# A two-layer graph/LSTM kernel: ScalarE instead of VectorE applies the first layer's normalisation, fused with its relu

## The chip, the cores and the metric

The kernel runs on one core of a Trainium2 chip. The metric is the device time of one execution in microseconds (us). The kernel before took 428.32 us, the median of 3 runs (428.17 to 431.04).

## The reference, cut to what matters

The input `x` is 64 batches of 128 rows (t) by 128 columns. Two layers with a residual follow each other; all of it is fp32.

```python
h = jnp.maximum(_layernorm(x, axis=-1), 0.0)          # the part that the change touches
x = x + _L0_gnn_ref(h, adj, Wg0, bg0, Wg1, bg1, Wih, Whh, bih, bhh)
h = jnp.maximum(_layernorm(x, axis=-1), 0.0)
x = x + _L1_gnn_ref(h, L1_W, adj, L1_bias)

# _L0_gnn_ref
h = relu(einsum('ts,bsh->bth', adj, x @ Wg0 + bg0))
h = relu(einsum('ts,bsh->bth', adj, h @ Wg1 + bg1))
for p in (1, 2, 3, 4):                                 # an LSTM over windows of p rows
    last = _lstm_last(Wih[p-1], Whh[p-1], bih[p-1], bhh[p-1], windows of p rows of h)
    h = h.at[:, every p-th row, :].set(last)
```

`_L1_gnn_ref` multiplies by three weight matrices, mixes the rows with the diagonal, the upper and the lower part of `adj`, and adds a bias.

## The kernel before, in words

**Groups and streams.** The 64 batches are worked off in 4 groups of 16. A group is split into two streams of 8 batches (s = 0 and 1) that alternate, so that one stream's matmuls run while the other stream's gates go through ScalarE and VectorE. `X` holds all of the input in SBUF; `H0` holds the normalised input of one group.

**Units.** The LSTM of a group is a list of 22 units (`UNITS`), k = 0 to 21, which all engines work off in the same order. A unit is one time step of one stream for one window length p: units 0 to 3 have p = 1, 4 to 7 p = 2, 8 to 13 p = 3 (336 columns) and 14 to 21 p = 4 (256 columns). Even k is stream 0 and odd k stream 1. Units 14 and 15 are the first steps of p = 4 and have three gates (input, cell, output); units 16 to 21 have four.

**What one unit does.** TensorE computes the gates into PSUM: first three matmuls per gate with the inputs `HH` and `HL` (high and low parts, L461, L462, L468), then, for a later step, three per gate with the state `SH` and `SL` (L477, L478, L481). The first L481 matmul of a unit waits for `SL` of the stream's previous unit. ScalarE applies sigmoid or tanh to each gate in turn (`GT`, L697), then, when VectorE has made the cell state `CS` (L808, or L811, L814 and L817), it takes its tanh (`TC`, L706). VectorE multiplies it with the output gate (`HT` or `HF`, L839) and makes the high part (L843) and the low part (L851). Every engine issues strictly in the order of its own program; nothing is rescheduled. VectorE calls `unit_cell` of units 1, 2 and 15 early (`CELL_EARLY`): for unit 15, the cell state comes ahead of `unit_low(14)`, which writes the `SL` that unit 16 needs.

**What is threaded between the units.** While group i is in its units, the layer norm of group i + 1 is prepared: VectorE takes the statistics after units 4 to 9 (L746), combines them at unit 10 (L753 to L765), and GpSimd makes `RS1` (one over the standard deviation, `rstd`, L320). Then VectorE applies it: at each of units 12 to 19 (`LN_APPLY_AT`), between `unit_cell` and `unit_hidden`, `norm_h0` (L771) computes (X + MINUS1) * RS1 for two batches. ScalarE applies the relu in place on eight batches at once (`relu_h0`, L632) after units 15 and 19 (`LN_RELU_AT`). Groups 0, 1 and 2 have a group to prepare (`more`); group 3 has none. For group 0's own batches, and for half of the second layer norm, ScalarE already makes normalisation and relu in one instruction per batch with `scale=RS` and `bias=SHIFT` (L674 and `norm_relu_h3`, L659).

**The last layer of the previous group.** From group 1 on, the second layer's work for group i - 1 is threaded into group i's units by a table (`Plan.at`): at (k, m), ahead of gate m of unit k, TensorE makes the mixed rows of one batch into PSUM (`last_uk`, L505 or L507 to L509), ScalarE copies them to `UK` (`copy_uk`, L665), and TensorE multiplies them by the weights (`last_out`, L522). All of these mixed rows go through one PSUM bank: at (15, 2) TensorE's `last_uk` of batch 15 waits until the copy of batch 14 is done, and ScalarE issues that copy at (15, 0), right after the tanh of unit 14. Group 0 has no such pieces.

## Time and profile before

| | |
|---|---|
| median of 3 runs | 428.32 us (428.17 to 431.04) |
| the profiled execution, its own time | 427.95 us |
| its span on the core | 425.6 us |
| mean granted TensorE clock | 0.992 of full speed |
| busy: TensorE matmul | 408.7 us (96%) |
| busy: VectorE | 328.8 us (77%) |
| busy: ScalarE | 279.9 us (66%) |
| busy: GpSimd | 48.2 us (11%) |

Busy time is the sum over an engine's instructions, without the gaps; a matmul's end is modelled, so a busy TensorE may still be kept from starting the next one on time. The span is what the trace covers; the execution's own time is 2.35 us longer. In the trace, PE is TensorE (PEld its weight loads), ACT is ScalarE, DVE is VectorE, POOL is GpSimd. Tiles appear under shortened names: H stands for H0 and H3, SHIFT for SHIFT1 and SHIFT2, RS for RS1 and RS2. Durations of neighbouring instructions on one engine overlap: where one starts less than its duration after the one before, the difference of the starts is what it occupies.

### The profile page before, as it was taken

Reading aid. Unit: us, or ns where it says so; the run is one execution under the profiler, and the core shown is the slowest. Engines: PE = TensorE matmul, PEld = TensorE weight load, DVE = VectorE, ACT = ScalarE, POOL = GpSimd, SP = SyncE. Lnnn points to the kernel's source line nnn. Section 1 sums busy time; section 2 is a strip of 40 time slices with the busy share of each in tenths; the row PEclk is TensorE's granted clock in tenths of the full one; section 3 lists DMA queues with packets and bytes.
Section 4 is the critical chain, followed back from the end, with each engine's and each line's share of the span. In section 5 each row is a group of like instructions: output and inputs, shape, how many; then the busy total and the mean of one; then the engine's idle time right before and its main releaser. Section 6 shows DMA issues by size and latency. Waiting matters only on the chain.

```text
span 425.6 us, 7802 instructions
## 1 busy us (share of the span) xinstructions
PE 408.7 (96%) x2594; PEld 366.6 (86%) x2594; DVE 328.8 (77%) x845; ACT 279.9 (66%) x566; POOL 48.2 (11%) x55
## 2 busy tenths in 40 slices
PE   8997989899999999999989999999999999999897
PEld 7785879898878889999867889999887889999787
DVE  5669888998886788887967678888888777767841
ACT  4667666765966576776766566767596676667542
POOL 3693002000200002000110001100110000000300
PEclk9998989999999999999999999999999999999999
DMA  7900000000001000000001000000000000000011
GB/s 217 375 28 1 2 0 2 1 2 0 2 19 39 14 0 15 1 20 2 0 2 37 32 0 12 1 18 0 1 2 19 27 0 14 0 20 0 9 55 63
DMA packets 6080, 11.16 MB, mean 26 GB/s; under 512 B 1056, under 2 KB 4768, under 8 KB 5536
## 3 DMA queue, kind: packets, MB, share of 16 engines
q1 hardware_dynamic: 6048, 10.77, 7.1%
q8 instruction: 16, 0.26, 0.2%
q14 instruction: 16, 0.13, 0.1%
HBM read 6.57 MB, written 4.19 MB: 25 GB/s over the span
## 4 chain that ended last, share of the span: by engine, by line
PE 82%; DVE 8%; ACT 4%; issue 3%; DMA 1%; POOL 1%; SPq 0%; DVEq 0%; ACTq 0%
PE PS L468 11%; PE PS L461 11%; PE PS L462 11%; PE PS L522 8%; PE PS L481 6%; PE PS L478 6%; PE PS L477 6%; PE PS L505 5%; PE PS L394 3%; PE PS L417 3%; PE PS L409 3%; PE PS L427 3%; ACT GT L697 2%; PE PS L491 1%; ACT TC L706 1%
## 5 line engine op out<-in xcount | busy, mean ns | idle before, releaser
L697 ACT ACTIVATE GT<-PS,BG 128x256 f32<-128x256 f32 (+2 forms) x312 | 159.1, 563 | 55.4 <-PE PS L481 31.2
L461 PE MATMUL PS<-HH,WIH 128*128 128x256 f32 (+2 forms) x312 | 109.9, 352 | 7.3 <-DVE HH L843 3.6
L468 PE MATMUL PS<-HL,WIH 128*128 128x256 f32 (+2 forms) x312 | 104.6, 335 | 0.4
L462 PE MATMUL PS<-HH,WIL 128*128 128x256 f32 (+2 forms) x312 | 104.2, 334 | 0.0
L706 ACT ACTIVATE TC<-CS 128x512 f32<-128x512 f32 (+2 forms) x88 | 45.1, 512 | 44.1 <-DVE CS L817 28.9
L461 PEld LDWEIGHTS PS<-HH,WIH 128*128 128x128 f32 x312 | 59.9, 192 | 12.2 <-DVE HH L843 4.3
L320 POOL TENSOR_TENSOR RS<-VE,NHALF 128x8 f32<-128x8 f32 (+2 forms) x15 | 26.5, 1766 | 350.9 <-DVE VE L765 350.9
L468 PEld LDWEIGHTS PS<-HL,WIH 128*128 128x128 f32 x312 | 59.8, 192 | 7.0 <-DVE HL L851 2.4
L462 PEld LDWEIGHTS PS<-HH,WIL 128*128 128x128 f32 x312 | 60.0, 192 | 3.5
L481 PE MATMUL PS<-SL,WHH 128*128 128x256 f32 (+2 forms) x192 | 59.8, 311 | 0.0
L478 PE MATMUL PS<-SH,WHL 128*128 128x256 f32 (+2 forms) x192 | 59.8, 311 | 0.0
L477 PE MATMUL PS<-SH,WHH 128*128 128x256 f32 (+2 forms) x192 | 59.7, 311 | 0.0
L522 PEld LDWEIGHTS PS<-WL,UK 128*128 128x128 f32 x384 | 50.9, 191 | 5.4
L522 PE MATMUL PS<-WL,UK 128*128 128x128 f32 x384 | 52.5, 275 | 0.0
L665 ACT ACTIVATE UK<-PS 128x384 f32<-128x384 f32 x64 | 31.0, 485 | 12.7 <-PE PS L509 8.9
L811 DVE TENSOR_TENSOR IC<-GT 128x256 f32<-128x256 f32 (+2 forms) x48 | 23.9, 498 | 19.1 <-ACT GT L697 18.9
L839 DVE TENSOR_TENSOR HF<-GT,TC 128x512 f32<-128x512 f32 (+2 forms) x40 | 24.6, 614 | 16.9 <-ACT TC L706 16.0
L478 PEld LDWEIGHTS PS<-SH,WHL 128*128 128x128 f32 x192 | 36.3, 189 | 1.3
L477 PEld LDWEIGHTS PS<-SH,WHH 128*128 128x128 f32 x192 | 36.3, 189 | 1.3
L481 PEld LDWEIGHTS PS<-SL,WHH 128*128 128x128 f32 x192 | 36.3, 189 | 1.3
L808 DVE TENSOR_TENSOR CS<-GT 128x512 f32<-128x512 f32 (+2 forms) x40 | 24.9, 622 | 12.4 <-ACT GT L697 10.2
L839 DVE TENSOR_TENSOR HT<-GT,TC 128x256 f32<-128x256 f32 (+2 forms) x48 | 23.8, 497 | 12.6 <-ACT TC L706 12.4
(81 smaller groups left out, 577.0 us busy)
## 6 DMA issues: line engine op xcount, KB each, us to landing
X<-x_tbd SPq DMA_DIRECT2D x3, 1024.0 KB, 12.5
out_tbd<-X SPq DMA_DIRECT2D x15, 192.0 KB, 1.9
X<-x_tbd SPq DMA_DIRECT2D x4, 256.0 KB, 4.5
WI<-wih_t SPq DMA_DIRECT2D x1, 1024.0 KB, 6.8
out_tbd<-X SPq DMA_DIRECT2D x7, 128.0 KB, 1.7
WH<-whh_t SPq DMA_DIRECT2D x1, 768.0 KB, 8.6
out_tbd<-X SPq DMA_DIRECT2D x1, 256.0 KB, 2.0
WL<-w_l SPq DMA_DIRECT2D x1, 192.0 KB, 7.0
```

Source lines behind the costliest of these rows:

```text
L320: pool.tensor_tensor(rs[:, lo:hi], ve[:, lo:hi], NHALF[:, lo:hi], ALU.pow).then_inc(done, 1)
L461: pe.matmul(dst, WIH[:, p - 1, cols], x_high, start=True, stop=False)
L462: pe.matmul(dst, WIL[:, p - 1, cols], x_high, start=False, stop=False)
L468: mm = pe.matmul(dst, WIH[:, p - 1, cols], x_low, start=False, stop=(j == 0))
L477: pe.matmul(dst, WHH[:, p - 2, cols], SH[:, s, 0:n], start=False, stop=False)
L478: pe.matmul(dst, WHL[:, p - 2, cols], SH[:, s, 0:n], start=False, stop=False)
L481: pe.matmul(dst, WHH[:, p - 2, cols], SL[:, s, 0:n], start=False, stop=True).then_inc(gate_mm, 1)
L522: mm = pe.matmul(as_batches(ps)[:, n - plan.chunks[c][0], :], UK[:, n % 4, k * T:(k + 1) * T], WL1[:, k, :], start=False, stop=(k == ADJ_P ...
L665: act.activation(UK[:, n % 4, :], ps[:, 0:ADJ_PARTS * T], ACT.Copy).then_inc(uk_sb, 1)
L697: act.activation(GT[:, s, q, 0:n], bank(s, q)[:, 0:n], ACT.Tanh if q == C else ACT.Sigmoid, bias=BG[:, 4 * (p - 1) + q:4 * (p - 1) + q + 1 ...
L706: act.activation(TC[:, s, 0:n], CS[:, s, 0:n], ACT.Tanh).then_inc(tanh_ready, 1)
L839: dve.tensor_tensor(full, o, tc, ALU.mult).then_inc(lstm_step, 1)
```

## The change

`norm_h0` on VectorE and `relu_h0` on ScalarE go. In their place ScalarE has `norm_relu_h0`: after the tanh of each of units 12 to 19 it makes relu(X * RS1 + SHIFT1) for two batches, one instruction per batch. GpSimd makes `SHIFT1` = MINUS1 * RS1 for the whole group with one more instruction behind its `RS1`. TensorE's wait ahead of the next group's first matmuls now counts batches (`h0_ready` is raised 16 times a group instead of 2). Nothing else moves.

```diff
-LN_RELU_AT = {15: 0, 19: 1}
...
             def group(i, more):
                 if more:
                     rstd(VE1, var1, 2 * (QUARTERS + i + 1), RS1, rs1, 0, G)
+                    pool.wait_ge(rs1, QUARTERS + i + 1)
+                    pool.tensor_tensor(SHIFT1[:, :], MINUS1[:, :], RS1[:, :], ALU.mult).then_inc(shift1, 1)
...
                 if not first:
-                    pe.wait_ge(h0_ready, STREAMS * (g - 1) + s + 1)
+                    pe.wait_ge(h0_ready, G * (g - 1) + HB * (s + 1))
...
         def _(act):
-            def relu_h0(s, g):
-
-                act.wait_ge(norm1, G * (g - 1) + HB * (s + 1))
-                part = H0[:, s * HB:(s + 1) * HB, :]
-                act.activation(part, part, ACT.Relu).then_inc(h0_ready, 1)
+            def norm_relu_h0(g, batches):
+
+                act.wait_ge(shift1, QUARTERS + g)
+                for b in batches:
+                    act.activation(H0[:, b, :], X[:, g * G + b, :], ACT.Relu, bias=SHIFT1[:, b:b + 1],
+                                   scale=RS1[:, b:b + 1]).then_inc(h0_ready, 1)
...
             def units(i, more, plan):
                 for k in range(len(UNITS)):
                     unit(k, i, plan)
-                    if more and k in LN_RELU_AT:
-                        relu_h0(LN_RELU_AT[k], i + 1)
+                    if more and k in LN_APPLY_AT:
+                        norm_relu_h0(i + 1, LN_APPLY_AT[k])
...
         def _(dve):
-            def norm_h0(g, ready, batches):
-
-                dve.wait_ge(rs1, ready)
-                for b in batches:
-                    dve.tensor_scalar(H0[:, b, :], X[:, g * G + b, :], MINUS1[:, b:b + 1], RS1[:, b:b + 1],
-                                      ALU.add, ALU.mult).then_inc(norm1, 1)
...
-                    if more and k in LN_APPLY_AT:
-                        norm_h0(i + 1, QUARTERS + i + 1, LN_APPLY_AT[k])
                     unit_hidden(k, i)
```

ScalarE in group 0, from the tanh of unit 13 (`TC`, 336 columns) to that of unit 16, before:

```order
L706 ACTIVATE TC<-CS 128x336
L697 ACTIVATE GT<-PS,BG 128x256 x3
L706 ACTIVATE TC<-CS 128x256
L697 ACTIVATE GT<-PS,BG 128x256 x3
L706 ACTIVATE TC<-CS 128x256
L632 ACTIVATE H<-H 128x1024
L697 ACTIVATE GT<-PS,BG 128x256 x4
L706 ACTIVATE TC<-CS 128x256
```

and the same stretch in the changed kernel, whose line numbers are by one or two different:

```order
L707 ACTIVATE TC<-CS 128x336
L632 ACTIVATE H<-X,SHIFT,RS 128x128 x2
L698 ACTIVATE GT<-PS,BG 128x256 x3
L707 ACTIVATE TC<-CS 128x256
L632 ACTIVATE H<-X,SHIFT,RS 128x128 x2
L698 ACTIVATE GT<-PS,BG 128x256 x3
L707 ACTIVATE TC<-CS 128x256
L632 ACTIVATE H<-X,SHIFT,RS 128x128 x2
L698 ACTIVATE GT<-PS,BG 128x256 x4
L707 ACTIVATE TC<-CS 128x256
```

Two small instructions stand behind every tanh, ahead of the next unit's gates; the large one behind unit 15 is gone. In groups 1 and 2 the same happens, and there the copy of batch 14 (`UK`) stands behind them too. ScalarE there, from the tanh of unit 14 on, before:

```order
L706 ACTIVATE TC<-CS 128x256 [waits cell_ready]
L664 REGISTER_ALU
L665 ACTIVATE UK<-PS 128x384 [waits uk_mm]
```

and changed, where the ISA rows are register work that the moving batch address needs:

```order
L707 ACTIVATE TC<-CS 128x256 [waits cell_ready]
L632 ISA [waits shift1]
L632 ACTIVATE H<-X,SHIFT,RS 128x128
L632 ISA
L632 ACTIVATE H<-X,SHIFT,RS 128x128
L665 REGISTER_ALU
L666 ACTIVATE UK<-PS 128x384 [waits uk_mm]
```

The copy, which came right behind the tanh, now has two instructions ahead of it. VectorE in group 0, from the high part of unit 13 (`HH`, L843) to that of unit 14, before:

```order
L843 CAST HH<-HF 128x42x8
L851 TENSOR_TENSOR HL<-HF,HH 128x42x8
L808 TENSOR_TENSOR CS<-GT 128x256
L771 TENSOR_SCALAR H<-X,MINUS,RS 128x128 x2
L839 TENSOR_TENSOR HT<-GT,TC 128x256
L843 CAST SH<-HT 128x256
L808 TENSOR_TENSOR CS<-GT 128x256
L851 TENSOR_TENSOR SL<-HT,SH 128x256
```

and changed:

```order
L837 CAST HH<-HF 128x42x8 [waits lstm_step]
L845 TENSOR_TENSOR HL<-HF,HH 128x42x8 [waits lstm_step]
L802 TENSOR_TENSOR CS<-GT 128x256 [waits gate_act]
L833 TENSOR_TENSOR HT<-GT,TC 128x256 [waits tanh_ready]
L837 CAST SH<-HT 128x256 [waits lstm_step]
L802 TENSOR_TENSOR CS<-GT 128x256 [waits gate_act]
L845 TENSOR_TENSOR SL<-HT,SH 128x256 [waits lstm_step]
```

The pair L771 is gone and nothing has changed places: the cell state of unit 15 (the second `CS`) still stands ahead of the `SL` of unit 14, and waits for ScalarE's gates (`gate_act`).

## Rows read from the trace of the kernel before

**Rows 1.** The page, busy time: busy us, share of the span, instructions.

```profile
PE 408.7 (96%) x2594; PEld 366.6 (86%) x2594; DVE 328.8 (77%) x845; ACT 279.9 (66%) x566; POOL 48.2 (11%) x55
```

**Rows 2.** The page, the chain that ended last, by engine.

```profile
PE 82%; DVE 8%; ACT 4%; issue 3%; DMA 1%; POOL 1%; SPq 0%; DVEq 0%; ACTq 0%
```

**Rows 3.** Groups of instructions by line and shape: busy us, mean ns | idle us before.

```profile
L632 ACT ACTIVATE H<-H 128x1024 f32<-128x1024 f32 x6 | 6.4, 1060 | 0.7 <-DVE H L771 0.4
L659 ACT ACTIVATE H<-X,SHIFT,RS 128x128 f32 x16 | 6.4, 481 | 0.5 <-POOL SHIFT L377 0.5
...
L771 DVE TENSOR_SCALAR H<-X,MINUS,RS 128x128 f32 x32 | 9.6, 341 | 0.0
```

**Rows 4.** Timeline of ScalarE in group 1: start us, length us, count.

```profile
209.71 0.86 ACT L659 ACTIVATE H<-X,SHIFT,RS 128x128 f32 x2
```

**Rows 5.** Line L659 alone: register work between its instructions, ns min/median/max.

```profile
L659 ACTq FUSED_REGOPS  x16: 51/55/60, 207.3 to 309.8; - x16
```

**Rows 6.** Timeline of ScalarE in group 1, the tanh of unit 12, then units 13 to 15.

```profile
169.71 0.48 ACT L706 ACTIVATE TC<-CS 128x336 f32<-128x336 f32 x1 [0.66 <-DVE CS L817]
...
173.41 0.48 ACT L706 ACTIVATE TC<-CS 128x336 f32<-128x336 f32 x1 [0.18 <-DVE CS L817]
173.80 1.19 ACT L697 ACTIVATE GT<-PS,BG 128x256 f32<-128x256 f32 x3
175.72 0.42 ACT L706 ACTIVATE TC<-CS 128x256 f32<-128x256 f32 x1 [0.73 <-DVE CS L808]
176.08 0.49 ACT L665 ACTIVATE UK<-PS 128x384 f32<-128x384 f32 x1
```

**Rows 7.** Timeline of VectorE in group 1, unit 14.

```profile
175.27 0.42 DVE L808 TENSOR_TENSOR CS<-GT 128x256 f32<-128x256 f32 x1
175.60 0.60 DVE L771 TENSOR_SCALAR H<-X,MINUS,RS 128x128 f32 x2
```

**Rows 8.** Timeline of TensorE, `last_uk` of batch 15 in group 1.

```profile
176.63 0.44 PE L507 MATMUL PS<-ADJ3H,H3H 128*128 128x384 f32 x1 [0.48 <-ACT UK L665]
```

**Rows 9.** Timeline of ScalarE in group 1, unit 17, the tanh of unit 19, the gates of unit 20.

```profile
183.84 1.57 ACT L697 ACTIVATE GT<-PS,BG 128x256 f32<-128x256 f32 x4 [0.32 <-PE PS L481]
186.00 0.42 ACT L706 ACTIVATE TC<-CS 128x256 f32<-128x256 f32 x1 [0.58 <-DVE CS L817]
...
191.73 0.42 ACT L706 ACTIVATE TC<-CS 128x256 f32<-128x256 f32 x1 [0.59 <-DVE CS L817]
...
193.21 1.55 ACT L697 ACTIVATE GT<-PS,BG 128x256 f32<-128x256 f32 x4
```

**Rows 10.** Timeline of VectorE in group 1, the low part of unit 19.

```profile
192.97 0.42 DVE L851 TENSOR_TENSOR SL<-HT,SH 128x256 fp32r<-128x256 f32 x1
```

**Rows 11.** Timeline of TensorE in group 1: unit 21's first L481, then the next group's first matmuls.

```profile
194.99 0.28 PE L481 MATMUL PS<-SL,WHH 128*128 128x256 f32 x1
...
196.18 1.95 PE L394 MATMUL PS<-ADJ,H 128*128 128x128 f32 x16
```

**Rows 12.** Timeline of ScalarE in group 0, the tanh of unit 13.

```profile
76.04 0.48 ACT L706 ACTIVATE TC<-CS 128x336 f32<-128x336 f32 x1 [0.66 <-DVE CS L817]
```

**Rows 13.** Timeline of VectorE in group 0, CS of unit 15, SL of unit 14.

```profile
79.52 0.42 DVE L808 TENSOR_TENSOR CS<-GT 128x256 f32<-128x256 f32 x1
79.86 0.42 DVE L851 TENSOR_TENSOR SL<-HT,SH 128x256 fp32r<-128x256 f32 x1
```

**Rows 14.** Timeline of TensorE in group 0: unit 15's start, first L481 of units 16 and 21.

```profile
77.49 0.39 PE L461 MATMUL PS<-HH,WIH 128*128 128x256 f32 x1 [1.65 <-DVE HH L843]
...
80.64 0.28 PE L481 MATMUL PS<-SL,WHH 128*128 128x256 f32 x1
...
95.00 0.28 PE L481 MATMUL PS<-SL,WHH 128*128 128x256 f32 x1
```

**Rows 15.** Timeline of GpSimd in group 1.

```profile
163.12 3.11 POOL L320 TENSOR_TENSOR RS<-VE,NHALF 128x16 f32<-128x16 f32 x1 [48.24 <-DVE VE L765]
...
207.06 0.20 POOL L377 TENSOR_TENSOR SHIFT<-MINUS,RS 128x8 f32<-128x8 f32 x1
```

More of the change, by code:

```diff
@@ L208, in program @@
         shift1 = sem("shift1")
-        norm1 = sem("norm1")
         h0_first = sem("h0_first")
```

## The prediction

> **What bounds the kernel now.** I read the page's busy times first, then the chain that ended last, then the groups by line and shape to price the instructions, and last the timelines of ScalarE, VectorE and TensorE around units 12 to 21, where the change works. TensorE is busy for 408.7 of 425.6 us [rows 1], and it holds 82% of the chain that ended last, ScalarE 4% and VectorE 8% [rows 2]. So a few us that leave VectorE give nothing by themselves, and a few that come to ScalarE cost nothing by themselves. What counts is whether TensorE's next matmul is held up by something that ScalarE does later than before. The reader should look for the places where TensorE already waits in this stretch: in group 1 for ScalarE's copy of batch 14, 0.48 us [rows 8] (group 2 has the same wait), and in group 0 for unit 13's high part, 1.65 us [rows 14]. Where TensorE waits for the very engine that gets work, there is no slack.
>
> **Removed.** Three groups have a successor. Each loses sixteen VectorE instructions of 341 ns, of which two take 0.60 us, thus eight pairs, and two ScalarE relu of 1.06 us [rows 3, 7]. The pairs stand between the cell state and the hidden state, where VectorE waits for the tanh anyway: the pair from 175.60 to 176.20 lies beside the tanh from 175.72 to 176.14 [rows 6, 7]. I count 0 gained, with the second rival below as the other end.
>
> **Added.** Sixteen ScalarE instructions per group. The nearest row is the same form on the same engine in the second layer norm: 481 ns each [rows 3], two in 0.86 us, so the second starts 0.38 us after the first [rows 4]. A pair then occupies 2 x 0.385 = 0.77 us. There is 55 ns of register work with each of them [rows 5], which the two in 0.86 us hide. Upper bound for a pair: no overlap and the register work in the open, 2 x (0.48 + 0.055) = 1.07 us. Lower bound: 0.76, two of the closest spacing that a row of this form shows. I take 0.77, because these rows are the same instruction in the same kind of loop. ScalarE gets 8 x 0.77 = 6.2 us per group and loses 2 x 1.06 = 2.1.
>
> Two instructions over 1024 columns become sixteen over 128: by [rows 3] an eighth of the columns still takes 0.48 of 1.06 us, so small pieces are dear here. The Trainium skill speaks against this change: "ScalarE: Activation LUTs", section "Rules for kernel authors", sends relu, add and mul to VectorE and not to ScalarE. By the durations the trace agrees, 341 ns there against 481 ns here; by that rule the change loses, and the third rival says how much it could lose at most. Whether TensorE waits for it the rule doesn't say.
>
> GpSimd gets one small product behind RS1. RS1 is out at 163.12 + 3.11 = 166.23 us, and a product of half the columns takes 0.20 us [rows 15]. Even at twice that, SHIFT1 is there by 166.8, and ScalarE first asks for it behind the tanh of unit 12, at 170.1 [rows 6]: no cost, and no gain either. TensorE's changed wait counts the sixteenth batch, ready behind unit 19, well before its use at 196.18 [rows 11]: no cost either, as long as ScalarE's lag stays as small as worked out below.
>
> **Groups 1 and 2: the copy of batch 14.** I walk ScalarE with the starts of group 1 [rows 6]. Behind unit 12 a pair takes up the time in which ScalarE waited for unit 13's gates, all but 0.05 us. So the tanh of unit 13 is at 173.46 instead of 173.41. The next instruction may start 0.39 later (173.80 - 173.41), and the pair pushes it by 0.77: gates of unit 14 at 174.62 instead of 173.80. The cell gate is the second of three that take 1.19 us together, so it ends some 0.83 later, at 175.45. VectorE makes CS from it at 175.48 instead of 175.27, when it had been held by its own earlier work [rows 7]. 0.42 later and 0.03 on, the tanh of unit 14 starts at 175.93 instead of 175.72. Then 0.36 and the second pair, 0.77: the copy starts at 177.06 instead of 176.08, that is 0.98 us later. The first delay is half swallowed by VectorE, the second not at all. TensorE's L507 already waits for this copy [rows 8], so it moves by the whole 0.98, and everything behind it in TensorE's program too. Group 2 repeats group 1. Together 1.96 us.
>
> **Groups 1 and 2: the lag that builds up afterwards,** measured against the shifted TensorE. ScalarE was idle for 0.32 us ahead of unit 17's gates [rows 9] and could have started 0.06 sooner still (a tanh takes 0.42, and the next starts 0.36 behind it [rows 6]). A pair of 0.77 there makes those gates 0.39 late. From gates to tanh are 186.00 - 183.84 = 2.16 us [rows 9], so with 0.36 and the pair a unit takes ScalarE 3.29 us. TensorE's unit takes 2.87 (24 matmuls; in these rows unit 20's gates would follow unit 17's by three of them, but for the relu). Each further unit adds 0.42: unit 18 is 0.81 late, unit 19 1.23. Unit 19's SL is out at 192.97 + 0.42 + 1.23 = 194.62 [rows 10], and TensorE needs it at 194.99 [rows 11]: 0.37 us of slack left, no stall. Behind unit 19 a pair replaces a longer relu, so unit 20's gates are at most 1 us late: 193.21 + 1.55 + 1.0 = 195.8, before the next group's matmuls at 196.18 ask for them. After that no pair follows, and ScalarE catches up. Cost 0; if the cover were gone, each 0.1 us more per pair costs unit 19's SL 0.3 us.
>
> **Group 0** has no pieces of the last layer. Here the late gates of unit 15 act through VectorE, which makes CS of unit 15 ahead of unit 14's SL. Tanh of unit 13 at 76.09 [rows 12], gates of unit 14 at 76.09 + 0.39 + 0.77 = 77.25, cell gate out at 78.08, CS at 78.11, tanh of unit 14 at 78.56, gates of unit 15 at 78.56 + 0.36 + 0.77 = 79.69, cell gate out at 80.52. So CS of unit 15 is at 80.55 instead of 79.52, SL of unit 14 stands 0.34 behind it as before [rows 13], at 80.89, and is out at 81.31. TensorE wanted it at 80.64 [rows 14]: a new stall of 0.69 us. Then the lag: tanh of unit 15 at 81.00, gates of unit 16 at 82.13, of unit 19 three periods of 3.29 later at 92.00, its tanh at 94.16, its SL 1.24 behind (192.97 against 191.73 [rows 9, 10]) at 95.40, out at 95.82. TensorE needs it at 95.00 + 0.69 = 95.69 [rows 14]: another 0.13. Group 0 costs 0.8 us.
>
> **Sum.** 0.8 + 2 x 0.98 = 2.8 us. The profiled execution took 427.95 us, 2.35 more than its span of 425.6; the same one would take 430.7 with a span of 428.4. The median of the runs shown lies 0.37 above the profiled one: 431.1 us, 0.6% slower.
>
> **The rivals.** First, slower by over 1%: a pair costs more than 0.77 us because the second instruction or the gates behind it don't overlap. At the upper bound of 1.07 the two pairs ahead of the copy make it 0.98 + 0.6 = 1.58 late; the lag is 0.69 at unit 17 and grows by 0.72, so unit 19's SL comes 0.5 after 194.99: 2.1 for each of groups 1 and 2. In group 0 unit 14's SL costs 1.3 and unit 19's another 1.3. Together 6.8 us: 435.1. Between 2.8 at 0.77 and 6.8 at 1.07 the bound of 1% (4.3 us) is passed at a pair of 0.88 us. For it: every pair stands behind a tanh and ahead of instructions that read PSUM, which the two of [rows 4] also do only in part. Against: they overlap all the same.
>
> Second, not slower: VectorE's pairs were what TensorE waited for, and their going gives back what ScalarE costs or more. If all of the waits in the stretch went (1.65 + 2 x 0.48 = 2.6 us), the time would be 425.7; if they only made up for my 2.8, 428.3. For it: VectorE starts its hidden states right behind a pair. Against: the tanh ends as the pair does, so its going releases nothing, and the copy of batch 14 doesn't depend on VectorE at all once the tanh is out.
>
> Third, all of the added occupancy counts, since ScalarE becomes the bound: 3 x (6.2 - 2.1) = 12.3 us, 440.6. That is the most that the rule of the skill named above could mean here. For it: with 3.29 us a unit ScalarE is slower than TensorE in units 16 to 19. Against: it is so for four units only, then it catches up, and over the span it is busy for 66% [rows 1].
>
> **How the numbers follow.** Chances: my forecast 0.68 (429 to 432.6), the dearer pair 0.18, no cost or a gain 0.11, all of it 0.03. The range of 428.6 to 434.2 reaches down into the second rival and up to a pair of about 1.0 us. A measurement of this kernel can tell about 1% from no change, here 4.3 us. Slower by more than that (above 432.6): the first and third rival and 0.01 of mine, 0.22. Faster by more than that needs more than all of TensorE's waits in the stretch: 0.03. Within 1%: 0.75.
>
> **What would show it.** In the profile of the changed kernel: pairs of 0.86 us on ScalarE behind each tanh of units 12 to 19; the L507 of batch 15 waiting for UK for about 1.4 us in groups 1 and 2; in group 0 a wait of TensorE for SL of about 0.7 us at unit 16; no idle time on ScalarE ahead of the gates of units 17 to 20; no new wait at the matmuls that open the next group; a span of 428.4. I am wrong if TensorE waits by more than 0.3 us for SL or SH in units 18 to 21 of groups 1 and 2, or if the copy's wait stays below 0.6.

## The result, and the profile after

| | before | changed |
|---|---|---|
| median of 20 runs each, us | 428.21 (425.75 to 431.04) | 431.48 (429.22 to 433.2) |
| profiled execution, us | 427.95 | 432.27 |
| its span, us | 425.6 | 430.1 |
| mean granted clock of that execution | 0.992 | 0.987 |

The ratio is 1.0065 (95% interval 1.005 to 1.008): the changed kernel is 0.65% slower, where 431.1 us was forecast. That is less than the 1% (4.3 us) that the prediction took as the least that can be told from no change, but the interval excludes no change. The times of both kernels spread with the granted clock, so medians and single spans are not the cleanest measure of some us. Grouped by mean granted clock, the executions at 0.992 have a mean span of 425.8 us before (44 executions, from the rounds of the experiments) and 428.6 changed (11): 2.8 us. Side by side in experiment 10 it is 425.8 (14) against 428.5 (seven). One execution of the kernel before, beside experiments 1 to 4, took 571.06 us at a clock of 0.656 and is left out everywhere. The changed kernel's profiled execution carries 1.5 us beside that, which the clock section at the end places.

The busy times and the chain's shares of the changed kernel's page, which answer to [rows 1, 2], and ScalarE's group for the new instructions:

```profile
PE 410.4 (95%) x2594; PEld 368.1 (86%) x2594; DVE 318.4 (74%) x797; ACT 290.7 (68%) x608; POOL 47.8 (11%) x58
PE 78%; DVE 10%; ACT 7%; issue 2%; DMA 1%; POOL 1%; ACTq 0%; SPq 0%; DVEq 0%
L632 ACT ACTIVATE H<-X,SHIFT,RS 128x128 f32 x32 | 13.9, 480 | 0.0
L632 ACT ACTIVATE H<-X,SHIFT,RS 128x128 f32<-128x128 f32 x16 | 6.9, 480 | 0.0
```

VectorE lost 10.4 us of busy time and ScalarE gained 10.8. No view of the chain shows a bound that moved: TensorE still holds 78% of it. But ScalarE's share went from 4 to 7%, and each of its 48 new instructions takes 480 ns, with no idle time ahead of it.

ScalarE in group 1 of the changed kernel, its timeline from unit 13's tanh to unit 21's gates, as [rows 6, 9] (start, duration, engine, instruction, in brackets the idle time ahead and what ended it):

```profile
174.30 0.48 ACT L707 ACTIVATE TC<-CS 128x336 f32<-128x336 f32 x1 [0.18 <-DVE CS L811]
174.69 0.86 ACT L632 ACTIVATE H<-X,SHIFT,RS 128x128 f32 x2
175.46 1.18 ACT L698 ACTIVATE GT<-PS,BG 128x256 f32<-128x256 f32 x3
176.76 0.42 ACT L707 ACTIVATE TC<-CS 128x256 f32<-128x256 f32 x1
177.08 0.86 ACT L632 ACTIVATE H<-X,SHIFT,RS 128x128 f32 x2
177.85 0.47 ACT L666 ACTIVATE UK<-PS 128x384 f32<-128x384 f32 x1
...
184.82 0.42 ACT L707 ACTIVATE TC<-CS 128x256 f32<-128x256 f32 x1 [0.59 <-DVE CS L811]
185.15 0.86 ACT L632 ACTIVATE H<-X,SHIFT,RS 128x128 f32 x2
185.92 1.55 ACT L698 ACTIVATE GT<-PS,BG 128x256 f32<-128x256 f32 x4
188.05 0.42 ACT L707 ACTIVATE TC<-CS 128x256 f32<-128x256 f32 x1 [0.58 <-DVE CS L811]
...
195.59 1.54 ACT L698 ACTIVATE GT<-PS,BG 128x256 f32<-128x256 f32 x4
```

From a pair's start to the next instruction it is 0.77 us at each of the three places (174.69 to 175.46, 177.08 to 177.85, 185.15 to 185.92). The copy of batch 14 (`UK`) starts at 177.85. From the tanh of unit 16 (184.82) to that of unit 17 it is 3.23 us, and the only idle time of ScalarE in a unit is the 0.58 in which it waits for the cell state.

TensorE in the changed kernel, its timeline at the places of [rows 8, 14]; the second line is group 1, the third group 2:

```profile
76.90 0.38 PE L461 MATMUL PS<-HH,WIH 128*128 128x256 f32 x1 [1.65 <-DVE HH L837]
...
178.37 0.44 PE L507 MATMUL PS<-ADJ3H,H3H 128*128 128x384 f32 x1 [1.33 <-ACT UK L666]
...
282.77 0.44 PE L507 MATMUL PS<-ADJ3H,H3H 128*128 128x384 f32 x1 [1.33 <-ACT UK L666]
```

The wait for the copy has grown from 0.48 to 1.33 us in both groups, and nothing new stands at units 18 to 21. In group 0 no wait for `SL` shows at unit 16 in this execution. Experiment 3's profile has one, and the clock section at the end says what differs.

**Where the time went.** The "graph stage" is the adjacency and weight matmuls that open a group, ahead of its units. I read the start of the same eight matmuls in each trace and take the differences. A is the first L461 of unit 15 in group 0 (behind its wait of 1.65), B the first L394 that follows (the opening of the next graph stage), C the first L461 of unit 9 in group 1 (behind a wait of 0.23), D the next L394 behind it; E is the third L505 of group 2 (it waits 1.56 for a copy before, 1.88 changed), F and G are C and D in group 2, H is the first L505 of the last group's own rows, near the end. In us:

| | A to B (group 0, units 15 to 21) | B to C | C to D (group 1) | D to E | E to F | F to G (group 2) | G to H |
|---|---|---|---|---|---|---|---|
| before | 18.71 | 58.41 | 41.57 | 22.60 | 37.60 | 41.52 | 103.56 |
| changed | 20.20 | 58.40 | 42.41 | 22.92 | 39.07 | 42.41 | 103.58 |

Groups 1 and 2 cost 0.84 and 0.89. The 1.49 of A to B and the 1.47 of E to F hold something else: the granted clock falls there, and it doesn't at the same places of the third and fifth experiments, which place group 0's cost at 0.72 + 0.23 = 0.95. The 0.32 of D to E is in this profile only: in experiment 10, the same kernel, D to E is 22.65.

### The profile page after: what moved, and what is told of

Same layout as the page of the kernel before. It is cut to its first block, busy times and chain, and to the rows that moved or that the text cites. A ratio compares the mean times of both kernels' runs of the same rounds, so it can differ in the third digit from the quotient of the medians.

```text
span 430.1 us, 7827 instructions
## 1 busy us (share of the span) xinstructions
PE 410.4 (95%) x2594; PEld 368.1 (86%) x2594; DVE 318.4 (74%) x797; ACT 290.7 (68%) x608; POOL 47.8 (11%) x58
## 4 chain that ended last, share of the span: by engine, by line
PE 78%; DVE 10%; ACT 7%; issue 2%; DMA 1%; POOL 1%; ACTq 0%; SPq 0%; DVEq 0%
PE PS L468 10%; PE PS L461 10%; PE PS L462 10%; PE PS L522 9%; PE PS L481 5%; PE PS L478 5%; PE PS L477 5%; PE PS L505 5%; ACT GT L698 4%; PE PS L427 3%; PE PS L394 3%; PE PS L417 3%; PE PS L409 3%; DVE CS L811 2%; DVE CS L808 2%
## 5 line engine op out<-in xcount | busy, mean ns | idle before, releaser
L461 PE MATMUL PS<-HH,WIH 128*128 128x256 f32 (+2 forms) x312 | 110.1, 353 | 8.0 <-DVE HH L837 7.5
L461 PEld LDWEIGHTS PS<-HH,WIH 128*128 128x128 f32 x312 | 60.3, 193 | 12.8 <-DVE HH L837 4.3
L481 PE MATMUL PS<-SL,WHH 128*128 128x256 f32 (+2 forms) x192 | 59.8, 311 | 0.0
L481 PEld LDWEIGHTS PS<-SL,WHH 128*128 128x128 f32 x192 | 36.3, 189 | 1.3
```

What stands on the lines that cost most here:

```text
L461: pe.matmul(dst, WIH[:, p - 1, cols], x_high, start=True, stop=False)
L481: pe.matmul(dst, WHH[:, p - 2, cols], SL[:, s, 0:n], start=False, stop=True).then_inc(gate_mm, 1)
```

## The experiments

Each ran in five rounds beside the kernel before, on the same chip as it (experiments 9 to 11 on another chip than 1 to 8; at a clock of 0.992 the kernel before has 425.8 us on both). "At equal clock" compares the mean spans of executions with the same mean granted clock. They are few in places, and the count stands beside each. "Period of ScalarE" below is the time from one unit's tanh to the next one's.

**1. The pair of unit 14 behind the copy** (groups 1 and 2 only).

```diff
+                    if plan is STEADY and k == 15 and m == 0:
+                        norm_relu_h0(i + 1, LN_APPLY_AT[14])
...
-                    if more and k in LN_APPLY_AT:
+                    if more and k in LN_APPLY_AT and not (plan is STEADY and k == 14):
```

> The changed kernel, but in the groups that carry last-layer pieces ScalarE issues the pair of unit 14 behind the copy of batch 14 and not ahead of it. Theory (ScalarE costs only where it stands ahead of something that TensorE waits for): the wait of TensorE's L507 for the copy shrinks from 1.33 us by one pair, 0.77, to 0.5 to 0.6 us in groups 1 and 2; the time falls by 1.5 us against the changed kernel, ratio to the kernel before about 1.003. Rival (all of ScalarE's added occupancy counts): nothing is removed, ratio stays at 1.0065. Rival (the loss is in the lag of units 16 to 19): stays at 1.0065 and TensorE shows waits there.

Measured: 430.44 us, ratio 1.0055 (1.0029 to 1.0082). TensorE at the copy in group 1:

```profile
179.44 0.44 PE L507 MATMUL PS<-ADJ3H,H3H 128*128 128x384 f32 x1 [0.58 <-ACT UK L666]
```

The wait is 0.58 instead of 1.33: the pair that stands directly ahead of the copy makes the 0.75 between them. C to D falls from 42.41 to 41.65, by 0.76. The median moved by less than that promises. Of this variant's 12 executions 9 had a mean clock of 0.988 or less, of the changed kernel's 12 of 32; at equal clock its span is 426.7 (0.992, two executions) and 428.3 (0.988, five), against 428.6 and 429.8 (three). So the work is 1.5 to 1.9 us shorter, and the clock takes a part of it back: the median fell by 1.0.

**2. All pairs away from the copy and from unit 15's gates.** The pairs of units 13 and 14 go behind units 11 and 15.

```diff
-LN_APPLY_AT = {12 + k: (2 * k, 2 * k + 1) for k in range(G // 2)}
+LN_APPLY_AT = {11: (0, 1), 12: (2, 3), 15: (4, 5, 6, 7), **{16 + k: (8 + 2 * k, 9 + 2 * k) for k in range(4)}}
```

> The changed kernel with the same sixteen instructions per group at other units: two batches behind each of units 11 and 12, none behind 13 and 14, four behind 15, two behind each of 16 to 19. Theory: no pair stands ahead of the copy of batch 14 (wait of L507 back at 0.5 us) and none delays the gates of units 14 and 15 (no stall for SL in group 0), ratio 1.000 to 1.001. Rival of the occupancy: the same 16 x 0.385 us are still on ScalarE, ratio 1.0065. Rival of the lag: the lag of units 16 to 19 is the same as before, ratio stays near 1.006.

Measured: 431.03 us, ratio 1.008 (1.0055 to 1.0106). The expectation was missed, and the median alone would say that the placement doesn't matter. The trace says otherwise: the copy's wait is down to what it was before,

```profile
179.59 0.44 PE L507 MATMUL PS<-ADJ3H,H3H 128*128 128x384 f32 x1 [0.42 <-ACT UK L666]
```

and no wait for `SL` is left. But 8 of its 9 executions had a clock of 0.988 or less. That made the ninth run necessary.

**3. VectorE's sixteen instructions put back.** They are issued at their old places, with their old operands and results, but write a part of Z that nothing reads; H0 still comes from ScalarE.

```diff
+            def norm_scr(g, ready, batches):
+
+                dve.wait_ge(rs1, ready)
+                for b in batches:
+                    dve.tensor_scalar(Z[:, b // HB, D * (b % HB):D * (b % HB) + D], X[:, g * G + b, :],
+                                      MINUS1[:, b:b + 1], RS1[:, b:b + 1], ALU.add, ALU.mult).then_inc(norm1, 1)
...
+                    if more and k in LN_APPLY_AT:
+                        norm_scr(i + 1, QUARTERS + i + 1, LN_APPLY_AT[k])
                     unit_hidden(k, i)
```

> The changed kernel with VectorE's sixteen instructions per group put back at their old places, writing to a tile that is dead at that time; nothing reads them. Theory (VectorE's relief gave nothing): equal to the changed kernel within 0.1%, ratio 1.006 to 1.007. Rival (VectorE's relief hid a part of ScalarE's cost): slower than the changed kernel, up to 1.012, with longer waits of TensorE for VectorE's SL or HH.

Measured: 430.75 us, ratio 1.007 (1.0044 to 1.0095); the profiled span is 428.4 at a clock of 0.992, where the changed kernel's mean at that clock is 428.6. With 11 us of VectorE work back (busy for 329.7 us, against 318.4), nothing became slower: their going had given back nothing. C to D is 42.42 (changed 42.41). This is also the trace in which group 0 can be read at an undisturbed clock. TensorE there, and the copy in group 1:

```profile
81.25 0.39 PE L482 MATMUL PS<-SL,WHH 128*128 128x256 f32 x1 [0.44 <-DVE SL L855]
...
178.43 0.44 PE L508 MATMUL PS<-ADJ3H,H3H 128*128 128x384 f32 x1 [1.34 <-ACT UK L667]
```

So the stall at unit 16 exists: 0.44 idle, and that matmul starts 3.77 behind A, where it was 3.15 before: 0.62. A to B is 19.43 against 18.71: 0.72. No lag is added to it at unit 21, whose first L482 uses unit 19's `SL`:

```profile
95.03 0.43 DVE L855 TENSOR_TENSOR SL<-HT,SH 128x256 fp32r<-128x256 f32 x1
95.72 0.28 PE L482 MATMUL PS<-SL,WHH 128*128 128x256 f32 x1
```

`SL` is out at 95.46, 0.26 ahead of its use. B to C is 58.64 against 58.41: 0.23 more, in the graph stage that follows, where the weight load of L418 (L417 before) waits 0.64 us for ScalarE's `Z` instead of 0.37.

**4. The copy of batch 14 ahead of unit 14's tanh,** which is an edit of the table that orders the pieces; the other copy of that row stays.

```diff
-        (13, 4): ((ADJP, 13),), (15, 0): both(14), (15, 2): both(15), (16, 1): ((OUTP, 15),)},
+        (13, 4): ((ADJP, 13),), (14, 3): ((ADJP, 14),), (15, 0): ((OUTP, 13),), (15, 2): both(15), (16, 1): ((OUTP, 15),)},
...
-        (13, 4): ((ADJP, 9),), (15, 0): both(10), (15, 2): both(11), (16, 1): ((OUTP, 11),)},
+        (13, 4): ((ADJP, 9),), (14, 3): ((ADJP, 10),), (15, 0): ((OUTP, 9),), (15, 2): both(11), (16, 1): ((OUTP, 11),)},
```

> The changed kernel with one entry of the table moved: the piece of batch 14 (in the last group batch 10) goes from ahead of unit 15's first gate to behind unit 14's last gate, so that ScalarE copies it ahead of unit 14's tanh and of the pair; TensorE's order is the same. Theory: the wait of L507 for the copy nearly goes (from 1.33 to under 0.2 us) in groups 1 and 2 and from 0.41 to under 0.1 in group 3, 2.6 us less for groups 1 and 2 at most, and ScalarE then lags by 1.2 us more behind TensorE in units 16 to 19, of which 0.1 to 0.4 us per group come back as waits for SL of unit 19; ratio 1.000 to 1.002. Rival of the occupancy: ratio stays at 1.006.

Measured: 428.63 us, ratio 1.0017 (0.9992 to 1.0041). ScalarE in group 1:

```profile
177.27 0.49 ACT L666 ACTIVATE UK<-PS 128x384 f32<-128x384 f32 x1
177.64 0.42 ACT L707 ACTIVATE TC<-CS 128x256 f32<-128x256 f32 x1
177.95 0.88 ACT L632 ACTIVATE H<-X,SHIFT,RS 128x128 f32 x2
```

The copy no longer stands behind tanh and pair, and no matmul shows a wait for it. But the weight load does, since the pair of unit 13 still makes gates and copy late:

```profile
177.81 0.19 PEld L507 LDWEIGHTS PS<-ADJ3H,H3H 128*128 128x128 f32 x1 [0.25 <-ACT UK L666]
```

C to D falls from 42.41 to 41.39; in experiment 7, with the same table edit and no pairs, it is 40.81. Group 0, which the edit doesn't reach, keeps its 0.72 (A to B 19.43). The span at 0.992 is 426.05 (six executions), which is 2.6 below the changed kernel.

**5. Unit 15's cell state behind unit 14's `SL`,** to take the wait for `SL` away from group 0.

```diff
-CELL_EARLY = (1, 2, 15)
+CELL_EARLY = (1, 2)
```

> The changed kernel with unit 15 taken out of the list of early cell states, so that VectorE makes the SL of unit 14 ahead of the CS of unit 15. Theory: the wait of TensorE for SL at unit 16 in group 0 (0.44 to 0.46 us in the traces where the clock did not hide it) goes, the two waits for the copy of batch 14 stay at 1.3 us; 0.5 us less than the changed kernel, which shows in the profile and hardly in the ratio (1.005 to 1.006). Rival (the stall comes from ScalarE's lag itself, not from the order on VectorE): the wait stays or moves to SH or SL of the same unit.

Measured: 430.97 us, ratio 1.0064 (1.0032 to 1.0095). The wait for `SL` at unit 16 is gone from the trace, and group 0 still costs 0.63 in A to B and 0.32 in B to C, 0.95 as in experiment 3. The 0.5 us that the expectation took off didn't come: at 0.992 the span is 428.45 (four), against 428.6. Taking the stall away gained nothing. ScalarE in this kernel, group 0:

```profile
75.67 0.87 ACT L632 ACTIVATE H<-X,SHIFT,RS 128x128 f32<-128x128 f32 x2
...
94.15 1.54 ACT L698 ACTIVATE GT<-PS,BG 128x256 f32<-128x256 f32 x4
```

The gates of unit 20 start 17.42 us behind A here (A is 76.73). In experiment 3, with the stall:

```profile
94.89 1.54 ACT L699 ACTIVATE GT<-PS,BG 128x256 f32<-128x256 f32 x4
```

that is 17.41 behind its A of 77.48. Before it was 16.41. ScalarE arrives equally late with and without the stall, since its own chain from unit 13 on sets it. And now TensorE reaches unit 21 early enough to be held there, its weight load by unit 19's `SL`, which it is not in experiment 3:

```profile
94.78 0.19 PEld L481 LDWEIGHTS PS<-SL,WHH 128*128 128x128 f32 x1 [0.16 <-DVE SL L845]
```

**6. A third instruction of the same form** behind units 16, 17 and 18, into a part of Z that nothing reads: extra work, to find out how much cover the lag has left.

```diff
+                        if k in (16, 17, 18):
+                            b = LN_APPLY_AT[k][0]
+                            act.activation(Z[:, 0, D * (k - 16):D * (k - 15)], X[:, (i + 1) * G + b, :], ACT.Relu,
+                                           bias=SHIFT1[:, b:b + 1], scale=RS1[:, b:b + 1]).then_inc(extra, 1)
```

> The changed kernel with one more instruction of the same form (0.385 us, into a tile that is dead at that time) behind each of units 16, 17 and 18. Theory (the lag of units 16 to 19 was covered with 0.37 us left in groups 1 and 2, with less than nothing left in group 0): 1.15 us more lag at unit 19, so 0.8 us per group in groups 1 and 2 and 1.1 in group 0, 2.7 us more than the changed kernel, ratio 1.012 to 1.013, with waits of TensorE for SL or SH of unit 19 at unit 21. Rival (ScalarE's occupancy is never on the path): no change, 1.0065. Rival (all occupancy counts, nothing was covered): 9 x 0.385 = 3.5 us more, 1.0145.

Measured: 435.53 us, ratio 1.0158 (1.0122 to 1.0194), six executions. TensorE now waits in the open at unit 21, in all three groups; the one of group 1:

```profile
198.90 0.39 PE L478 MATMUL PS<-SH,WHH 128*128 128x256 f32 x1 [0.23 <-DVE SH L844]
```

C to D and F to G are 43.15, both 0.74 above the changed kernel, where 0.8 was forecast; A to B is 0.76 above it. Three instructions are 1.16 us of ScalarE at 0.385 each; 0.74 of them reach TensorE within the units, so 0.4 us of cover was left there, as the prediction had it (0.37).

But most of the covered part is paid later, which the expectation didn't have. The stages behind the units are longer too: B to C by 0.36, G to H by 0.35, and D to E is 23.21, against 22.92 in the changed kernel's profile and 22.65 in experiment 10's. At a clock of 0.992 the span is 432.0 (two executions), 3.4 above the changed kernel. The theory had 2.7 and the rival "all occupancy counts" 3.5, so by the total the rival is nearer; by the stages it is wrong about where. By these two executions nearly all of the added time of ScalarE was paid, about two thirds of it in the units and the rest in the stage behind them.

**7. The kernel before, with only the table edit of experiment 4.**

> The kernel before with only the piece of batch 14 (batch 10 in the last group) moved behind unit 14's last gate, so that its copy comes ahead of unit 14's tanh. Theory: TensorE's three waits of 0.48, 0.42 and 0.41 us go, 1.2 us less than before at most, ratio 0.997 to 0.998. Rival (the copy delays the tanh and with it the chain of unit 14): ratio 1.000 or above.

Measured: **425.88 us, ratio 0.9944 (0.9917 to 0.9971)**, faster than the kernel before. ScalarE in group 1:

```profile
173.90 1.19 ACT L697 ACTIVATE GT<-PS,BG 128x256 f32<-128x256 f32 x3
174.97 0.50 ACT L665 ACTIVATE UK<-PS 128x384 f32<-128x384 f32 x1
175.82 0.42 ACT L706 ACTIVATE TC<-CS 128x256 f32<-128x256 f32 x1 [0.34 <-DVE CS L808]
```

The copy fits between the gates and the tanh, where ScalarE has nothing to do. C to D is 40.81, 0.76 below before; F to G 0.72, G to H 0.70 below. At a clock of 0.992 the span is 423.8 (six executions), 1.9 below before. Each of the three waits showed 0.41 to 0.48 us of idle TensorE and was worth 0.70 to 0.76; the expectation had counted the idle time alone. The rest is in rows beside it. TensorE's weight load before, in group 1:

```profile
176.62 0.19 PEld L507 LDWEIGHTS PS<-ADJ3H,H3H 128*128 128x128 f32 x1 [0.68 <-ACT UK L665]
```

The load itself had waited 0.68, and the matmul behind it takes 0.44 [rows 8], while in this experiment, unheld, it takes 0.34:

```profile
176.08 0.34 PE L507 MATMUL PS<-ADJ3H,H3H 128*128 128x384 f32 x1
```

Here each such wait cost 0.28 to 0.30 us beside its idle time.

**8. Experiment 2's placement and the table edit together.**

> The changed kernel with the pairs moved as in the run e2_pairs_moved and the copy of batch 14 moved as in e4_copy_ahead_of_tanh. Theory: no wait for the copy, no stall for SL of unit 14; 1.2 us less than the kernel before at an equal granted clock, ratio 0.997 to 0.999 if the clock drops as often as in the kernel before. In e2 the waits were gone as forecast, but the ratio was 1.008 and the mean granted clock 0.984 to 0.988 against 0.992 of the kernel before: if that belongs to the placement of the pairs, it repeats here and the ratio is 1.003 to 1.005; if it was that job's accident, the clocks are 0.992 again.

Measured: 427.37 us, ratio 0.9983 (0.9959 to 1.0006). At a clock of 0.992 its span is 424.7 (seven executions): 1.0 below before, 0.9 above experiment 7. In groups 1 and 2 that difference is not at the pairs behind units 15 to 19. C to D is 41.01, 0.2 above experiment 7, and all of it is there when unit 15 starts (20.53 behind C, against 20.32): with pairs behind both unit 11 and unit 12, the tanh of unit 13 is 0.2 late, and with it the `HH` that TensorE waits for. D to E is 0.19 above experiment 7; A to B holds a fall of the clock here and can't be read.

**9. Experiment 2 again, and 10. the changed kernel again,** with no edit to either, to see whether the median of experiment 2 was chance.

> The same kernel as e2_pairs_moved, to tell whether its extra clock drops belong to it. In e2 the profile had no wait that the kernel before has not, and all of its 3 us sat in two more drops of TensorE's clock (mean clock 0.984 to 0.988). If the drops belong to the placement of the pairs: clock again 0.984 to 0.988 in most runs and ratio 1.006 to 1.008. If they were chance: 0.992 in most runs and ratio 1.000 to 1.003; at an equal clock the span is within 0.5 us of the kernel before in either case.

> The changed kernel itself, beside the others on the same chip. Theory: ratio 1.006 to 1.008; at a mean clock of 0.992 its span is 2.8 us above that of the kernel before, of which 0.9 us lie in group 0 and 0.9 in each of groups 1 and 2.

Measured: 430.45 us, ratio 1.0048 (1.0023 to 1.0073), and 431.06 us, ratio 1.0073 (1.0042 to 1.0103). The intervals overlap: by their medians the two placements can't be told apart. By the stages they can: C to D and F to G are 41.71 (twice) in the ninth and 42.42 in the tenth, A to B 19.17 in the ninth, against 19.43 in experiment 3. And at a clock of 0.992 the spans are 427.1 (three) and 428.5 (seven). The placement of experiment 2 is worth 1.4 us at equal clock, and its executions get the lower clock in 8 of 12 cases. It is still 1.3 above before, where the expectation had at most 0.5: 0.46 in A to B and 0.31 in B to C, without a stall at unit 16, and 0.14 to 0.22 in each of C to D, D to E and F to G.

**11. Seven of the changed kernel's sixteen instructions ahead of a tanh instead of behind it,** with the table edit. The sixteen are the same; one each of units 12 and 16 to 21 is issued between the gates and the wait for the cell state. The other nine still stand behind a tanh: two at unit 11, one at 12, four at 15, one each at 16 and 17.

```diff
-LN_APPLY_AT = {12 + k: (2 * k, 2 * k + 1) for k in range(G // 2)}
+LN_APPLY_AT = {11: (0, 1), 12: (3,), 15: (4, 5, 6, 7), 16: (9,), 17: (11,)}
+LN_AHEAD_OF_TANH = {12: (2,), 16: (8,), 17: (10,), 18: (12,), 19: (13,), 20: (14,), 21: (15,)}
...
+                if plan is not LATE and k in LN_AHEAD_OF_TANH:
+                    norm_relu_h0(i + 1, LN_AHEAD_OF_TANH[k])
```

> ScalarE makes the same sixteen instructions per group, placed by where it stands idle: two behind unit 11's tanh, one ahead of and one behind unit 12's, four behind unit 15's, one ahead of each tanh of units 16 to 21, one more behind those of 16 and 17; the copy of batch 14 ahead of unit 14's tanh. Theory (the place decides, not the amount): ScalarE's idle time between a unit's last gate and its tanh, 0.58 us, takes an instruction of 0.385 us for nothing, so no lag builds up; no wait for the copy; the span equals that of e7_before_copy_moved at an equal clock (423.8 us at 0.992), ratio 0.994 to 0.997. Rival (the amount counts): ratio 1.000 or above. Rival (VectorE's 12 us less of work give something once ScalarE is out of the way): below e7, 0.993 or less.

Measured: **426.0 us, ratio 0.9943 (0.992 to 0.9966)**. The page's busy times, and ScalarE in group 1:

```profile
PE 407.9 (96%) x2594; PEld 366.4 (87%) x2594; DVE 316.9 (75%) x797; ACT 291.9 (69%) x608; POOL 47.8 (11%) x58
```

```profile
182.44 0.48 ACT L633 ACTIVATE H<-X,SHIFT,RS 128x128 f32 x1
182.86 1.57 ACT L699 ACTIVATE GT<-PS,BG 128x256 f32<-128x256 f32 x4
184.31 0.50 ACT L633 ACTIVATE H<-X,SHIFT,RS 128x128 f32 x1
185.01 0.42 ACT L710 ACTIVATE TC<-CS 128x256 f32<-128x256 f32 x1 [0.20 <-DVE CS L814]
185.34 0.48 ACT L633 ACTIVATE H<-X,SHIFT,RS 128x128 f32 x1
185.72 1.57 ACT L699 ACTIVATE GT<-PS,BG 128x256 f32<-128x256 f32 x4
187.17 0.50 ACT L633 ACTIVATE H<-X,SHIFT,RS 128x128 f32 x1
187.88 0.42 ACT L710 ACTIVATE TC<-CS 128x256 f32<-128x256 f32 x1 [0.20 <-DVE CS L814]
188.59 1.57 ACT L699 ACTIVATE GT<-PS,BG 128x256 f32<-128x256 f32 x4 [0.29 <-PE PS L482]
```

ScalarE is as busy as in the changed kernel (291.9 against 290.7 us), with the same 608 instructions, and by 188.59 it waits for TensorE again. In each of these units one instruction of 0.48 to 0.50 us lies between the last gate and the tanh, in the time that ScalarE had spent waiting for `CS` (0.58 in the changed kernel, 0.20 left). Stage by stage the kernel is experiment 7: A to B 18.73, C to D 40.80, F to G 40.83. At a clock of 0.992 the spans are 423.7 (six executions) and 423.8 (six). So the change's own work costs nothing at the right places, and the 12 us that it takes off VectorE are worth nothing there either. It beats both kernels, by the table edit alone. With that edit in all of them, the sixteen instructions cost 2.2 us at the changed kernel's places (experiment 4 against 7), 0.9 at experiment 2's (experiment 8) and nothing here.

## Why the prediction was right, and where it wasn't

**A pair takes 0.77 us: right.** It is 0.77 at every place read, ahead of gates and copies that read PSUM too, and the rival of a pair of 1.07 falls.

**The relief of VectorE is worth 0: right.** Experiment 3 gives the work back without a loss, experiment 11 keeps it away without a gain. The rival in which VectorE gives the cost back falls.

**The copy of batch 14: right in mechanism, 0.1 us a group too dear.** The forecast wait was about 1.4, the measured one 1.33. The term was 0.98 a group; C to D and F to G rose by 0.84 and 0.89. The term that was mis-sized is the one of 0.98: the copy's wait grew by 0.85 (0.48 to 1.33). The walk had unit 13's tanh 0.05 late, but it is where it was (18.80 behind C in both kernels, since it waits for `CS`), and it had the next instruction 0.36 behind unit 14's tanh, where the pair starts after 0.32 (176.76 to 177.08). That is 0.09 of the 0.1. Experiment 1 puts the pair of unit 14 at 0.75 of the wait. In experiment 9, with the copy's wait as before, C to D is 0.14 above before: next to nothing else in the group costs time.

**The lag of units 16 to 19 is covered in groups 1 and 2: right, with a longer period than measured.** The period is 3.23 us (forecast 3.29). VectorE's `SL` of unit 19, [rows 10], is out at 196.15 in the changed kernel, group 1:

```profile
195.73 0.42 DVE L845 TENSOR_TENSOR SL<-HT,SH 128x256 fp32r<-128x256 f32 x1
```

and TensorE's first L481 of unit 21, which uses it, starts at 196.72, 0.57 later, where 0.37 of slack was forecast. Experiment 6 measured the cover from the other side: three more instructions used up 0.4 us of it within the units, and then TensorE waited at unit 21, for `SH` first. It also showed that such a lag goes on into the next graph stage, which the prediction looked at only for its first matmuls. In the changed kernel itself that came to nothing in groups 1 and 2 (experiment 10: D to E 0.05 above before, G to H 0.03). The third rival falls, since all of the added occupancy would have been 12.3 us. The Trainium skill, "ScalarE: Activation LUTs", section "Rules for kernel authors", would keep such work on VectorE. The durations agree (480 ns against 341), and the changed kernel is slower; but experiment 11 has the same instructions on ScalarE at no cost, so here the place in the queue decides, which the rule doesn't ask for.

**Group 0: the sum was near (0.8 forecast, 0.95 measured), its parts were not.** The walk gave a stall of 0.69 at unit 16 (its own figures, 81.31 and 80.64, give 0.67) and 0.13 of lag at unit 21. In experiment 3 the stall moves TensorE by 0.62 at unit 16 and A to B by 0.72. The 0.13 isn't there: the walk had unit 19's `SL` out at 95.82 and it is out at 95.46, half of the difference being the period of 3.29 instead of 3.23 taken three times. The 0.23 that makes up for it lies behind the units, where the prediction had nothing.

Experiment 5 adds what the numbers of the walk allowed but nobody drew from them: stall and lag are two bounds side by side. It took the stall away and left 0.95, since ScalarE, busy from unit 13's tanh on but for its waits for `CS`, reaches unit 20 a us late either way. The expectation of that experiment should have asked what becomes late once the stall is gone.

**"After that no pair follows, and ScalarE catches up": wrong in group 0, by 0.2 to 0.3 us.** ScalarE is still a us late at units 20 and 21, and the delay reaches the next graph stage: B to C is 0.23 more in experiment 3, 0.32 in experiment 5. The sentence was written for groups 1 and 2, where it holds; the step that failed is that group 0 got no price at all behind unit 21.

**The sum** of 2.8 us agrees with the stages: 0.95 + 0.84 + 0.89 = 2.7, and with the spans at equal clock (2.8). A part that was too small in group 0 and one that was too large in groups 1 and 2 nearly cancel. That is luck in part. The median rose by 3.3 instead of 2.8; at equal clock it is 2.8, so what is left goes with the clock.

## What to carry to other kernels

On an engine that works its queue in order, an added instruction is priced by what stands behind it: with the table edit in both, the same sixteen instructions cost 2.2 us two by two behind each tanh, and nothing once seven of them stood between gates and tanh, where the engine waits for another one anyway, and the other nine were spread over other units. Look for that idle time before moving work to an engine "with room", and look for a copy that stands behind a wait it doesn't need: that edit of the table was the only gain in this case. A lag that no wait shows can be paid in the next stage (experiment 6), so read the stages behind it too. When a stall is taken out, walk the late engine to the end of the stage before counting the gain, since a second bound may lie beside it.

## What the runs showed of the hardware that wasn't expected

**A few tenths of idle TensorE are worth more than they show.** Three waits of 0.41 to 0.48 us gave 0.70 to 0.76 us each when they went (experiment 7).

**The clock makes a spread larger than this change.** TensorE's granted clock falls from full (2.4 GHz) to half (1.2) behind some of its waits, and not behind the same ones in each execution. The changed kernel's windows of its profiled execution (window, its length, busy time and count of TensorE, its weight loads, VectorE, ScalarE and GpSimd, then the granted clock, DMA share and GB/s):

```profile
76.00:80.00 4.00, 3.06 (x14) 2.85 (x15) 2.61 (x7) 3.87 (x11) 0.00 (x0) 0.70 0.00 0
80.00:84.00 4.00, 4.00 (x32) 4.00 (x31) 2.98 (x8) 2.94 (x8) 0.00 (x0) 0.88 0.00 0
216.00:220.00 4.00, 2.95 (x12) 1.90 (x11) 1.07 (x3) 2.73 (x5) 0.68 (x1) 1.00 0.01 4
220.00:224.00 4.00, 3.17 (x10) 2.58 (x11) 3.59 (x10) 2.86 (x6) 0.00 (x0) 0.62 0.01 2
```

The clock is down behind the 1.65 us for `HH` at 76.90, and again behind this wait, where a group begins:

```profile
220.83 1.55 PE L505 MATMUL PS<-ADJ,H 128*128 128x384 f32 x2 [1.88 <-ACT UK L666]
```

The profiled execution of before kept its clock at both places:

```profile
76.00:80.00 4.00, 2.48 (x18) 2.27 (x19) 3.86 (x13) 3.10 (x9) 0.00 (x0) 1.00 0.00 0
```

Its clock fell between 56 and 60 us instead, where the changed kernel's didn't:

```profile
56.00:60.00 4.00, 3.32 (x11) 3.09 (x12) 3.86 (x11) 2.41 (x6) 0.00 (x0) 0.58 0.00 0
```

The changed kernel's second drop is the 1.5 us of E to F by which the changed kernel's profile is longer than its mean at a clock of 0.992. The first one hides the stall for `SL` at unit 16: `SL` is out 3.72 behind A both here and in experiment 3, but TensorE asks for it 4.66 behind A here. The profiles that show that drop and have no extra work come to 78.6 us from A to C (five of them, 78.55 to 78.63); experiment 6, with its third instructions, has 79.7. Without the drop it is 77.1 before, 78.0 to 78.1 in experiments 3 to 5 and 77.9 in experiment 9. With the drop A to C is 1.5 above before, no more than the drop at E to F adds by itself, so the drop seems to hide all of group 0's 0.95 and not only the stall. No profile of the kernel before has the drop at that place, so this is not shown.

In the kernel before, one step of 0.004 in the mean clock goes with 1.0 to 1.7 us of span (423.7 at 1.0, 425.8 at 0.992, 427.4 at 0.988 and 0.987, 428.4 at 0.984 and 0.983). The kernel before was at 0.988 or less in 20 of 89 executions, the changed one in 12 of 32, experiments 1, 2 and 9 in 25 of 33, experiments 7 and 11 in 3 of 24. Why a placement of the pairs that shortens TensorE's waits for the copy is given the lower clock more often stays open; no run separates it.
